# A recommendation model on one core: the last head in two halves, the last pairs in portions, spare matmuls behind the last products, and later waits for the gathers

## The chip, the core and the metric

The kernel runs on one core of one Trainium2 chip. A core has four engines that compute, each with its own stream of instructions: TensorE (PE), VectorE (DVE), ScalarE (ACT) and GpSimd (POOL). A fifth, SyncE (SP), only starts transfers here. They are kept in order by semaphores alone. The metric is the device time of one execution in microseconds (us). Before the change it is 152.27 us, the median of three runs (151.87 to 156.4).

## What is computed

512 samples each have 13 dense numbers and 26 table indices. Two dense layers make one vector of 128 from the dense numbers, a lookup in 26 tables makes 26 more. The dot products of all pairs of the 27 vectors, with the first vector itself, go through three layers to one probability. All is fp32.

```python
h = relu(dense_x @ bw1 + bb1)
x_bottom = relu(h @ bw2 + bb2)
sparse_embs = emb_tables[field_idx, sparse_x]
combined = concatenate([x_bottom[:, None, :], sparse_embs], axis=1)
interactions = einsum('bfd,bgd->bfg', combined, combined)
x_final = concatenate([x_bottom, interactions[:, rows, cols]], axis=-1)   # rows, cols: triu_indices(27, k=1)
t = relu(x_final @ tw1 + tb1)
t = relu(t @ tw2 + tb2)
return sigmoid(t @ tw3 + tb3)
```

## The kernel before

The 512 x 26 table rows are fetched in 104 chunks of 128 rows. Thirteen chunks make a group of 64 samples; there are 8 groups, 0 to 7, and `LAST` is 7. Two groups make a turn of 128 samples (`TURN`), and each turn ends in a head: layers 1 to 3.

**GpSimd** starts one indirect transfer per chunk, a gather, on line 189. Chunk c has its own place in `rows`, so no gather waits for a free buffer. Still, from chunk 4 on (`LEAD`) a gather waits until chunk c - 4 is transposed (line 188).

**PE** transposes each chunk through an identity (line 326) into one of two PSUM banks, `rows_T`; ahead of each transpose stands a matmul whose result is overwritten and never read (line 323). A group's 13 chunks are handled in units: 4, 3, 3, 3, and in the last group 4, 3, 3, 2, 1. Behind the transposes of a unit come the products of the unit before (`multiply`, line 342). One product takes a quad, 4 samples at once, 104 columns. A group has 16 quads in two batches of 8; batch h goes to `products[h]`, two PSUM banks of 4 quads each. An fp32 matmul shows as two passes in the trace, a transpose as one.

**DVE** copies the transposed chunks to `fields` (`fields_in`, line 224). The pairs, blocks of 32 partitions of the products, are brought to `pairs` by `take_pairs` (line 166) in 16 small copies per batch, 8 on DVE (quadrants 0 and 1) and 8 on ACT (quadrants 2 and 3). Three of four have 56 elements a partition, the fourth 40.

**The head** of a turn is layer 1 (line 351 for the dense vector, then 7 matmuls, line 357, with the pairs), `relu1` on ACT (271), layer 2 (366), `relu2` (277), layer 3 (372), `sigmoid` (283). The heads of turns 0 to 2 run inside the next turn's first group, layer 1 behind `multiply(group, 0)`. That of turn 3 stands behind all products. SP stores the 512 results when the last sigmoid is done.

Each engine runs its instructions strictly in the order in which its function below writes them. In the last group DVE takes the pairs of batch 0 between the fields of units 1 and 2 (lines 242 to 247).

Of the kernel before, what the change touches and what calls it, by code (L numbers as in the profile page):

```python
# [15 lines left out]
P = 128  # L16
BATCH = 512
# [40 lines left out]


TURN = 2 * GROUP  # L60


def evacuation_pieces(c0, c1):
# [29 lines left out]
def dlrm(nc, index_base, dense_bw1, weights, pair_weights, table, out):  # L93
# [7 lines left out]
    with ctx:  # L101
# [50 lines left out]

            return NU * group + u

        def take_pairs(copy, group, h, quadrants):

            src = products[h][:, :].rearrange("p (b c) -> p b c", c=BANK)[
                :, :, 0:BANK_QUADS * QUAD * SPARSE].rearrange(
                "p b (q s g) -> p s g b q", s=QUAD, g=SPARSE)
            a = group % 2  # L160
            dst = pairs[:, :, a * GROUP:(a + 1) * GROUP].rearrange(
                "p g (h b q s) -> p h s g b q", h=BATCHES, q=BANK_QUADS, s=QUAD)
            for s in quadrants:
                for j in range(SPLIT):
                    g0, g1 = j * PART, min((j + 1) * PART, SPARSE)
                    last = copy(dst[SLOT * j:SLOT * (j + 1), h, s, 0:g1 - g0],  # L166
                                src[SLOT * s:SLOT * (s + 1), s, g0:g1])
            return last

        block = ctx.enter_context(nc.Block())  # L170
# [1 line left out]
        @block.sync  # L172
        def _(sp):
            sp.dma_start(raw[:, :], index_base).then_inc(index_loaded, 16)
            sp.dma_start(w[:, :], weights).then_inc(weights_loaded, 16)
            sp.dma_start(wp[:, :, :], pair_weights).then_inc(pair_weights_loaded, 16)
            sp.wait_ge(probs_ready, ROUNDS)
# [15 lines left out]

        @block.vector
        def _(dve):
# [51 lines left out]
            pairs_in(LAST, 1)  # L247

        @block.scalar
        def _(act):  # L250
# [17 lines left out]
            def relu1(t):  # L268

                act.wait_ge(top1_made, t + 1)  # L270
                nc.scalar.activation(top1[:, :], top1_ps[:, 0:TURN], ACT.Relu,  # L271
                                     bias=w[:, TB1:TB1 + 1]).then_inc(top1_ready, 1)

            def relu2(t):

                act.wait_ge(top2_made, t + 1)
                nc.scalar.activation(top2[:, :], top2_ps[0:T2, 0:TURN], ACT.Relu,  # L277
                                     bias=w[0:T2, TB2:TB2 + 1]).then_inc(top2_ready, 1)

            def sigmoid(t):  # L280

                act.wait_ge(logits_made, t + 1)
                nc.scalar.activation(probs[:, t * TURN:(t + 1) * TURN], top2_ps[0:1, TURN:2 * TURN],  # L283
                                     ACT.Sigmoid, bias=w[0:1, TB3:TB3 + 1]).then_inc(probs_ready, 1)

            for t in range(ROUNDS):
# [4 lines left out]
                if t > 0:  # L291
                    sigmoid(t - 1)
                pairs_in(2 * t, 1)
                pairs_in(2 * t + 1, 0)
                pairs_in(2 * t + 1, 1)
            relu1(ROUNDS - 1)
            relu2(ROUNDS - 1)
            sigmoid(ROUNDS - 1)

        @block.tensor  # L300
        def _(pe):
# [9 lines left out]
                                       hidden[:, h, :], start=(h == 0), stop=(h == HH - 1))  # L311
            ins.then_inc(bottom_made, 1)

            def transposes(group, u):


# [3 lines left out]
                    pe.wait_ge(fields_ready, v - 1)  # L320
                for k in range(c0, c1):
                    c = group * GROUP_CHUNKS + k
                    nc.tensor.matmul(rows_T[v % 2][:, (k - c0) * P:(k - c0 + 1) * P], w[:, IDENT:IDENT + P],  # L323
                                     w[:, IDENT:IDENT + P], start=True, stop=True)
                    pe.wait_ge(gathered[c], 16)
                    nc.tensor.transpose(rows_T[v % 2][:, (k - c0) * P:(k - c0 + 1) * P],  # L326
                                              rows[:, c, :], w[:, IDENT:IDENT + P]).then_inc(transposed, 1)

            def multiply(group, u):

# [16 lines left out]
            def layer1(t):  # L347

                if t > 0:
                    pe.wait_ge(top1_ready, t)  # L350
                nc.tensor.matmul(top1_ps[:, 0:TURN], w[:, TW1X:TW1X + T1],  # L351
                                 fields[:, t * TURN:(t + 1) * TURN, 0], start=True, stop=False)
                for h in range(BATCHES):
                    pe.wait_ge(taken_dve[h], 2 * (t + 1))
                    pe.wait_ge(taken_act[h], 2 * (t + 1))
                for g in range(PART):
                    ins = nc.tensor.matmul(top1_ps[:, 0:TURN], wp[:, g, :], pairs[:, g, :],  # L357
                                           start=False, stop=(g == PART - 1))
                ins.then_inc(top1_made, 1)

            def layer2(t):

                pe.wait_ge(top1_ready, t + 1)
                if t > 0:
                    pe.wait_ge(probs_ready, t)
                nc.tensor.matmul(top2_ps[0:T2, 0:TURN], w[:, TW2:TW2 + T2], top1[:, :],  # L366
                                 start=True, stop=True).then_inc(top2_made, 1)

            def layer3(t):

                pe.wait_ge(top2_ready, t + 1)
                nc.tensor.matmul(top2_ps[0:1, TURN:2 * TURN], w[0:T2, TW3:TW3 + 1], top2[:, :],  # L372
                                 start=True, stop=True).then_inc(logits_made, 1)

            transposes(0, 0)
# [31 lines left out]
            layer3(ROUNDS - 1)  # L407


def pair_weight_order():  # L410
# [51 lines left out]
```

## Time and profile before

| | us |
|---|---|
| median of 3 runs | 152.27 |
| the profiled execution | 152.51 |
| its span, first to last instruction | 150.7 |
| PE busy / DVE / ACT / POOL | 106.8 / 56.8 / 39.5 / 98.7 |
| mean granted clock of PE | 0.909 of full |

Times in the trace count from the start of the span. Full speed of PE is 2.4 GHz, a granted clock of 0.50 is 1.2 GHz. PEld is the weight load of PE, which overlaps the matmuls. In a row of the timeline stand start, length, engine, line, operation, output and inputs with their shapes, how many instructions are merged, and in brackets how long the engine was idle before and who released it.

### The profile page before, as it was taken

How to read it: one execution, taken by the hardware profiler on the slowest of the kernel's cores; microseconds unless marked ns; L12 is line 12 of the kernel's file. 1: busy time of each engine (PE TensorE's matmuls, PEld its weight loads, DVE VectorE, ACT ScalarE, POOL GpSimd, SP SyncE). 2: the span in 40 equal slices, each digit the busy share in tenths (PEclk: the TensorE clock that was granted, in tenths of full speed). 3: DMA queues.
4: the chain of work that ended last, by engine and by line, in shares of the span. 5: the costliest groups of instructions: out<-in, count | busy, mean ns of one | idle time of the engine just before them, and what ended most of it. 6: DMA issues, size and time to landing. Idle time of an engine off the chain costs nothing.

```text
span 150.7 us, 1841 instructions
## 1 busy us (share of the span) xinstructions
PE 106.8 (71%) x656; PEld 87.6 (58%) x656; DVE 56.8 (38%) x219; ACT 39.5 (26%) x145; POOL 98.7 (65%) x108
## 2 busy tenths in 40 slices
PE   2993666656589978866666975566499969578682
PEld 1352555555459957755555954455498849468470
DVE  1702153262606261535326160716135442561600
ACT  3320031040404160313104160505013430450402
POOL 0727777777777777777777777777777777771000
PEclk9999999999955997799999999999959986975859
DMA  4311112221121222212121211221112122211000
GB/s 125 137 35 35 52 52 52 57 52 52 54 52 52 52 59 52 54 52 52 52 52 57 52 52 52 52 52 52 57 52 52 52 54 52 57 52 35 0 0 1
DMA packets 3797, 7.80 MB, mean 52 GB/s; under 512 B 1854, under 2 KB 1854, under 8 KB 3788
## 3 DMA queue, kind: packets, MB, share of 16 engines
q0 software_dynamic: 3328, 6.82, 17.2%
q1 hardware_dynamic: 434, 0.82, 1.8%
q8 instruction: 5, 0.08, 0.2%
q10 hardware_dynamic: 26, 0.04, 0.1%
q14 instruction: 4, 0.03, 0.1%
HBM read 7.67 MB, written 0.00 MB: 51 GB/s over the span
## 4 chain that ended last, share of the span: by engine, by line
POOL 41%; PE 23%; issue 15%; DMA 15%; DVE 3%; ACT 1%; DVEq 0%
POOL rows L189 41%; DMA rows<-table,row_index 14%; PE products L342 6%; PE top_ps L357 5%; PE rows_T L326 3%; PE rows_T L305 3%; PE rows_T L323 2%; PE products L310 2%; DVE pairs L166 2%; DMA db<-dense_bw 1%; DVE fields L224 1%; PE top_ps L351 1%; PE top_ps L372 0%; PE top_ps L366 0%; ACT top L271 0%
## 5 line engine op out<-in xcount | busy, mean ns | idle before, releaser
L189 POOL DMA_INDIRECT rows<-table,row_index x104 | 98.5, 947 | 37.4 <-issue 26.5
L326 PE MATMUL rows_T<-w,rows 128*128 128x128 f32 x104 | 34.5, 331 | 34.3 <-DMA rows<-table,row_index 33.9
L166 ACT COPY pairs<-products 32x56 f32<-32x56 f32 (+1 forms) x128 | 31.1, 243 | 82.1 <-PE products L342 80.8
L224 DVE COPY fields<-rows_T 128x494 f32<-128x494 f32 (+6 forms) x83 | 22.3, 319 | 73.9 <-PE rows_T L326 73.7
L323 PE MATMUL rows_T<-w 128*128 128x128 f32 x208 | 44.6, 308 | 0.0
L326 PEld LDWEIGHTS rows_T<-w,rows 128*128 128x128 f32 x104 | 16.3, 157 | 44.5 <-DMA rows<-table,row_index 44.3
L323 PEld LDWEIGHTS rows_T<-w 128*128 128x128 f32 x208 | 38.5, 228 | 1.0 <-issue 1.0
L342 PE MATMUL products<-fields 128*128 128x104 f32 x256 | 37.6, 294 | 2.0 <-DVE fields L224 2.0
L342 PEld LDWEIGHTS products<-fields 128*128 128x128 f32 x256 | 35.1, 211 | 4.3 <-DVE fields L224 3.0
L166 DVE COPY pairs<-products 32x56 f32<-32x56 f32 (+1 forms) x128 | 30.9, 241 | 9.1 <-PE products L342 7.2
L357 PE MATMUL top_ps<-pairs,wp 128*128 128x128 f32 x56 | 8.5, 313 | 1.9 <-DVE pairs L166 1.9
L357 PEld LDWEIGHTS top_ps<-pairs,wp 128*128 128x128 f32 x56 | 8.2, 226 | 2.3 <-issue 2.2
L305 PE MATMUL rows_T<-db 13*128 13x512 f32 x4 | 3.8, 1096 | 2.8 <-DMA db<-dense_bw 2.8
L271 ACT ACTIVATE top<-top_ps,w 128x128 f32<-128x128 f32 x4 | 1.5, 368 | 12.9 <-PE top_ps L357 12.9
L310 PE MATMUL products<-hidden,w 128*128 128x512 f32 x4 | 3.8, 1101 | 0.0
L305 PEld LDWEIGHTS rows_T<-db 13*128 13x128 f32 x4 | 1.2, 318 | 3.9 <-DMA db<-dense_bw 2.8
L310 PEld LDWEIGHTS products<-hidden,w 128*128 128x128 f32 x4 | 1.2, 324 | 2.5 <-issue 2.0
L351 PE MATMUL top_ps<-fields,w 128*128 128x128 f32 x8 | 2.4, 389 | 0.0
L283 ACT ACTIVATE probs<-top_ps,w 1x128 f32<-1x128 f32 x4 | 1.4, 358 | 3.6 <-PE top_ps L372 3.6
L213 DVE MEMSET fields<- 128x2560 f32 x1 | 2.2, 2192 | 0.5 <-issue 0.5
L277 ACT ACTIVATE top<-top_ps,w 64x128 f32<-64x128 f32 x4 | 1.4, 362 | 3.5 <-PE top_ps L366 3.5
L257 ACT ACTIVATE hidden<-rows_T,w 128x512 f32<-128x512 f32 x2 | 1.4, 688 | 3.1 <-PE rows_T L305 3.1
(16 smaller groups left out, 10.1 us busy)
## 6 DMA issues: line engine op xcount, KB each, us to landing
rows<-table,row_index POOLq DMA_INDIRECT x104, 2.5
wp<-pair_weights SPq DMA_DIRECT2D x1, 448.0 KB, 3.7
w<-weights SPq DMA_DIRECT2D x1, 291.5 KB, 3.0
raw<-index_base SPq DMA_DIRECT2D x1, 58.5 KB, 2.2
db<-dense_bw ACTq DMA_DIRECT2D x1, 39.0 KB
out<-probs SPq DMA_DIRECT2D x1, 2.0 KB
```

What stands on the lines that cost most here:

```text
L166: last = copy(dst[SLOT * j:SLOT * (j + 1), h, s, 0:g1 - g0], src[SLOT * s:SLOT * (s + 1), s, g0:g1])
L189: nc.gpsimd.indirect_dma_start(rows[:, c, :], None, table, bass.IndirectOffsetOnAxis(row_index[:, group, k:k + 1], 0)).then_inc(gathered[c ...
L213: nc.vector.memset(fields[:, :, SPARSE + 1:SLOT], 0.0)
L224: ins = nc.vector.tensor_copy(fields[:, b:b + n, 1 + f:1 + f + nf], rows_T[v % 2][:, col:col + n * nf].rearrange("p (n f) -> p n f", f=nf))
L271: nc.scalar.activation(top1[:, :], top1_ps[:, 0:TURN], ACT.Relu, bias=w[:, TB1:TB1 + 1]).then_inc(top1_ready, 1)
L305: nc.tensor.matmul(rows_T[h][:, 0:BATCH], db[:, BATCH + h * P:BATCH + (h + 1) * P], db[:, 0:BATCH], start=True, stop=True).then_inc(hidden ...
L310: ins = nc.tensor.matmul(products[0][:, 0:BATCH], w[:, BW2 + h * EMB:BW2 + (h + 1) * EMB], hidden[:, h, :], start=(h == 0), stop=(h == HH ...
L323: nc.tensor.matmul(rows_T[v % 2][:, (k - c0) * P:(k - c0 + 1) * P], w[:, IDENT:IDENT + P], w[:, IDENT:IDENT + P], start=True, stop=True)
L326: nc.tensor.transpose(rows_T[v % 2][:, (k - c0) * P:(k - c0 + 1) * P], rows[:, c, :], w[:, IDENT:IDENT + P]).then_inc(transposed, 1)
L342: ins = nc.tensor.matmul(products[h][:, col:col + n], four, four[:, :, 1:1 + SPARSE], start=True, stop=True)
L351: nc.tensor.matmul(top1_ps[:, 0:TURN], w[:, TW1X:TW1X + T1], fields[:, t * TURN:(t + 1) * TURN, 0], start=True, stop=False)
L357: ins = nc.tensor.matmul(top1_ps[:, 0:TURN], wp[:, g, :], pairs[:, g, :], start=False, stop=(g == PART - 1))
```

## The change

Four things. The wait of the gathers begins at chunk 8 instead of 4; it still asks for chunk c - 4. The heads are listed in `HEADS`: three of 128 samples, then one for group 6 and one for group 7, 64 samples each. Head 3 (group 6) now runs inside the last group: layer 1 behind the transposes of unit 1, layer 2 behind `multiply(LAST, 1)`, layer 3 behind `multiply(LAST, 2)`. In the last group, the pairs come in three steps: batch 0 whole, then the first bank of batch 1 (4 quads; one quadrant on DVE, three on ACT), then its second bank. And four matmuls that nobody reads stand behind the last products.

```diff
+HEADS = [(0, TURN), (TURN, 2 * TURN), (2 * TURN, 3 * TURN), (3 * TURN, 3 * TURN + GROUP),
+         (3 * TURN + GROUP, BATCH)]
...
-                if c >= LEAD:
+                if c >= 2 * LEAD:
                     pool.wait_ge(transposed, c - LEAD + 1)
...
+            def last_pairs_in(n, h, quadrants, b0, b1):
+
+                dve.wait_ge(multiplied, BATCHES * LAST + n)
+                take_pairs(nc.vector.tensor_copy, LAST, h, quadrants, b0, b1).then_inc(taken_dve[h], 1)
+
             fields_in(LAST, 1)
-            pairs_in(LAST, 0)
             fields_in(LAST, 2)
+            last_pairs_in(1, 0, (0, 1), 0, 2)
             fields_in(LAST, 3)
+            last_pairs_in(2, 1, (0,), 0, 1)
             fields_in(LAST, 4)
-            pairs_in(LAST, 1)
+            last_pairs_in(3, 1, (0, 1), 1, 2)
...
-            relu1(ROUNDS - 1)
-            relu2(ROUNDS - 1)
-            sigmoid(ROUNDS - 1)
...
+            relu1(3)
+            last_pairs_in(1, 0, (2, 3), 0, 2)
+            relu2(3)
+            sigmoid(3)
+            last_pairs_in(2, 1, (1, 2, 3), 0, 1)
+            last_pairs_in(3, 1, (2, 3), 1, 2)
+            relu1(4)
+            relu2(4)
+            sigmoid(4)
...
+            def keep_busy(spare, n):
+
+                for _ in range(n):
+                    nc.tensor.matmul(spare, w[:, IDENT:IDENT + P], w[:, IDENT:IDENT + P],
+                                     start=True, stop=True)
...
-                    if at == BATCH_QUADS - 1:
+                    if at == BATCH_QUADS - 1 or (group, h, at) == (LAST, 1, BANK_QUADS - 1):
                         ins.then_inc(multiplied, 1)
...
             multiply(LAST, 0)
             transposes(LAST, 1)
+            layer1(3)
             multiply(LAST, 1)
+            layer2(3)
             transposes(LAST, 2)
             multiply(LAST, 2)
+            layer3(3)
             transposes(LAST, 3)
             transposes(LAST, 4)
             multiply(LAST, 3)
             multiply(LAST, 4)
-            layer1(ROUNDS - 1)
-            layer2(ROUNDS - 1)
-            layer3(ROUNDS - 1)
+            keep_busy(rows_T[0][:, 0:P], 4)
+            layer1(4)
+            layer2(4)
+            layer3(4)
```

How this stands in the engines' streams. DVE, the end of the last group: `fields` copies come from `rows_T`, `pairs` copies from `products`. Before, from the fields of unit 1 on:

```order
L224 COPY fields<-rows_T 128x12
L166 COPY pairs<-products 32x7x8 x3
L166 COPY pairs<-products 32x5x8
L166 COPY pairs<-products 32x7x8 x3
L166 COPY pairs<-products 32x5x8
L224 COPY fields<-rows_T 128x14
L224 COPY fields<-rows_T 128x14x26
L224 COPY fields<-rows_T 128x6
L224 COPY fields<-rows_T 128x20
```

After, from the fields of unit 2 on:

```order
L227 COPY fields<-rows_T 128x6
L169 COPY pairs<-products 32x7x8 x3
L169 COPY pairs<-products 32x5x8
L169 COPY pairs<-products 32x7x8 x3
L169 COPY pairs<-products 32x5x8
L227 COPY fields<-rows_T 128x20
L227 COPY fields<-rows_T 128x9x26
L227 COPY fields<-rows_T 128x2
L169 COPY pairs<-products 32x7x4 x3
L169 COPY pairs<-products 32x5x4
L227 COPY fields<-rows_T 128x24
L227 COPY fields<-rows_T 128x4x26
```

The pairs of batch 0 moved from ahead of unit 2's fields to behind them, and four copies of half size stand between the fields of the last two units.

PE behind the last transpose of unit 1 in the last group (L342 of before and L372 of after are products, L323 and L342 of after the matmuls that nobody reads). Before:

```order
L326 MATMUL rows_T<-w,rows 128x128
L342 MATMUL products<-fields 128x104 x4
L323 MATMUL rows_T<-w 128x128
L326 MATMUL rows_T<-w,rows 128x128
L323 MATMUL rows_T<-w 128x128
```

After:

```order
L357 MATMUL rows_T<-w,rows 128x128
L383 MATMUL top_ps<-fields,w 128x64
L390 MATMUL top_ps<-pairs,wp 128x64 x7
L372 MATMUL products<-fields 128x104 x4
L400 MATMUL top_ps<-top,w 64x64
L342 MATMUL rows_T<-w 128x128
L357 MATMUL rows_T<-w,rows 128x128
```

Eight matmuls of layer 1 and one of layer 2 now stand ahead of the next transpose. The end of PE's stream, before:

```order
L326 MATMUL rows_T<-w,rows 128x128
L342 MATMUL products<-fields 128x104 x4
L351 MATMUL top_ps<-fields,w 128x128
L357 MATMUL top_ps<-pairs,wp 128x128 x7
L366 MATMUL top_ps<-top,w 64x128
L372 MATMUL top_ps<-top,w 1x128
```

And after:

```order
L357 MATMUL rows_T<-w,rows 128x128
L372 MATMUL products<-fields 128x104 x4
L342 MATMUL rows_T<-w 128x128 x4
L383 MATMUL top_ps<-fields,w 128x64
L390 MATMUL top_ps<-pairs,wp 128x64 x7
L400 MATMUL top_ps<-top,w 64x64
L407 MATMUL top_ps<-top,w 1x64
```

The head's matmuls are as many as before with half the columns, and four spare matmuls stand ahead of them.

## Rows read from the trace of the kernel before

**Rows 1.** The page, chain that ended last, share of the span by engine.

```profile
POOL 41%; PE 23%; issue 15%; DMA 15%; DVE 3%; ACT 1%; DVEq 0%
```

**Rows 2.** The list of waits, GpSimd: us in total, times, longest.

```profile
POOL rows L189 <- PE rows_T L326: 7.5, 16, 2.5
```

**Rows 3.** The timeline of the start: start, us, engine, line, operation, wait.

```profile
7.74 0.95 POOL L189 DMA_INDIRECT rows<-table,row_index  x1 [0.30 <-issue]
...
10.35 1.15 ACT L260 ACTIVATE fields<-products,w 128x512 f32<-128x512 f32 x1 [3.02 <-PE products L310]
...
11.18 0.95 POOL L189 DMA_INDIRECT rows<-table,row_index  x1 [2.50 <-PE rows_T L326]
...
13.74 0.33 PE L326 MATMUL rows_T<-w,rows 128*128 128x128 f32 x1 [1.61 <-DMA rows<-table,row_index]
```

**Rows 4.** The timeline in group 6, with the head of turn 2.

```profile
113.99 0.33 PE L326 MATMUL rows_T<-w,rows 128*128 128x128 f32 x1 [0.34 <-DMA rows<-table,row_index]
...
114.16 1.04 PE L342 MATMUL products<-fields 128*128 128x104 f32 x8
...
115.46 1.74 PE L357 MATMUL top_ps<-pairs,wp 128*128 128x128 f32 x14
...
117.26 0.27 PE L326 MATMUL rows_T<-w,rows 128*128 128x128 f32 x1
...
117.81 0.95 POOL L189 DMA_INDIRECT rows<-table,row_index  x1 [0.47 <-PE rows_T L326]
```

**Rows 5.** The timeline of the last group and the last head.

```profile
131.13 0.33 PE L326 MATMUL rows_T<-w,rows 128*128 128x128 f32 x1 [1.23 <-DMA rows<-table,row_index]
...
133.41 2.05 DVE L166 COPY pairs<-products 32x56 f32<-32x56 f32 x8 [1.23 <-PE products L342]
...
135.44 0.95 POOL L189 DMA_INDIRECT rows<-table,row_index  x1 [0.30 <-issue]
135.49 0.69 DVE L224 COPY fields<-rows_T 128x14 f32<-128x14 f32 x3
...
139.62 0.99 DVE L224 COPY fields<-rows_T 128x20 f32<-128x20 f32 x5 [3.44 <-PE rows_T L326]
...
140.23 1.22 PE L342 MATMUL products<-fields 128*128 128x104 f32 x8
...
141.49 2.01 DVE L166 COPY pairs<-products 32x56 f32<-32x56 f32 x8 [0.87 <-PE products L342]
...
143.76 3.25 PE L357 MATMUL top_ps<-pairs,wp 128*128 128x128 f32 x14 [1.87 <-DVE pairs L166]
147.05 0.37 ACT L271 ACTIVATE top<-top_ps,w 128x128 f32<-128x128 f32 x1 [3.55 <-PE top_ps L357]
...
147.47 0.43 PE L366 MATMUL top_ps<-top,w 128*64 128x128 f32 x2 [0.46 <-ACT top L271]
...
148.77 0.36 ACT L283 ACTIVATE probs<-top_ps,w 1x128 f32<-1x128 f32 x1 [0.47 <-PE top_ps L372]
```

**Rows 6.** Groups of instructions by shape: count, us busy, mean ns, idle before.

```profile
L166 DVE COPY pairs<-products 32x56 f32<-32x56 f32 x96 | 23.8, 248 | 8.7 <-PE products L342 7.2
...
L166 DVE COPY pairs<-products 32x40 f32<-32x40 f32 x32 | 7.1, 222 | 0.4
...
L257 ACT ACTIVATE hidden<-rows_T,w 128x512 f32<-128x512 f32 x2 | 1.4, 688 | 3.1 <-PE rows_T L305 3.1
...
L224 DVE COPY fields<-rows_T 128x24 f32<-128x24 f32 x1 | 0.2, 183 | 0.1
```

**Rows 7.** Stretches of the end: length, busy by engine, granted clock, DMA, GB/s.

```profile
133.70:140.40 6.70, 5.47 (x25) 4.67 (x24) 3.06 (x15) 1.69 (x7) 2.08 (x3) 0.50 0.12 29
130.20:133.60 3.40, 1.69 (x13) 1.50 (x14) 0.87 (x4) 0.19 (x1) 2.55 (x3) 1.00 0.21 57
140.50:143.80 3.30, 1.43 (x11) 1.07 (x11) 2.04 (x9) 1.93 (x8) 0.00 (x0) 1.00 0.00 0
143.90:147.00 3.10, 3.10 (x14) 2.82 (x14) 0.00 (x0) 0.00 (x0) 0.00 (x0) 0.50 0.00 0
```

More of the change, by code:

```diff
@@ L153, in unit_number, with take_pairs @@
             return NU * group + u
-        def take_pairs(copy, group, h, quadrants):
+        def take_pairs(copy, group, h, quadrants, b0=0, b1=BATCH_QUADS // BANK_QUADS):
             src = products[h][:, :].rearrange("p (b c) -> p b c", c=BANK)[
@@ L165, in take_pairs @@
                     g0, g1 = j * PART, min((j + 1) * PART, SPARSE)
-                    last = copy(dst[SLOT * j:SLOT * (j + 1), h, s, 0:g1 - g0],
-                                src[SLOT * s:SLOT * (s + 1), s, g0:g1])
+                    last = copy(dst[SLOT * j:SLOT * (j + 1), h, s, 0:g1 - g0, b0:b1],
+                                src[SLOT * s:SLOT * (s + 1), s, g0:g1, b0:b1])
             return last
@@ L176, in _ @@
             sp.dma_start(wp[:, :, :], pair_weights).then_inc(pair_weights_loaded, 16)
-            sp.wait_ge(probs_ready, ROUNDS)
+            sp.wait_ge(probs_ready, len(HEADS))
             sp.dma_start(out, probs[:, :]).then_inc(stored, 16)
@@ L266, in pairs_in, with relu1, relu2, sigmoid @@
                 take_pairs(nc.scalar.copy, group, h, (2, 3)).then_inc(taken_act[h], 1)
-            def relu1(t):
-                act.wait_ge(top1_made, t + 1)
-                nc.scalar.activation(top1[:, :], top1_ps[:, 0:TURN], ACT.Relu,
+            def relu1(i):
+                n = HEADS[i][1] - HEADS[i][0]
+                act.wait_ge(top1_made, i + 1)
+                nc.scalar.activation(top1[:, 0:n], top1_ps[:, 0:n], ACT.Relu,
                                      bias=w[:, TB1:TB1 + 1]).then_inc(top1_ready, 1)
-            def relu2(t):
-                act.wait_ge(top2_made, t + 1)
-                nc.scalar.activation(top2[:, :], top2_ps[0:T2, 0:TURN], ACT.Relu,
+            def relu2(i):
+                n = HEADS[i][1] - HEADS[i][0]
+                act.wait_ge(top2_made, i + 1)
+                nc.scalar.activation(top2[:, 0:n], top2_ps[0:T2, 0:n], ACT.Relu,
                                      bias=w[0:T2, TB2:TB2 + 1]).then_inc(top2_ready, 1)
-            def sigmoid(t):
-                act.wait_ge(logits_made, t + 1)
-                nc.scalar.activation(probs[:, t * TURN:(t + 1) * TURN], top2_ps[0:1, TURN:2 * TURN],
+            def sigmoid(i):
+                lo, hi = HEADS[i]
+                act.wait_ge(logits_made, i + 1)
+                nc.scalar.activation(probs[:, lo:hi], top2_ps[0:1, TURN:TURN + hi - lo],
                                      ACT.Sigmoid, bias=w[0:1, TB3:TB3 + 1]).then_inc(probs_ready, 1)
@@ L322, in transposes @@
                     c = group * GROUP_CHUNKS + k
-                    nc.tensor.matmul(rows_T[v % 2][:, (k - c0) * P:(k - c0 + 1) * P], w[:, IDENT:IDENT + P],
-                                     w[:, IDENT:IDENT + P], start=True, stop=True)
+                    block_T = rows_T[v % 2][:, (k - c0) * P:(k - c0 + 1) * P]
+                    keep_busy(block_T, 1)
                     pe.wait_ge(gathered[c], 16)
-                    nc.tensor.transpose(rows_T[v % 2][:, (k - c0) * P:(k - c0 + 1) * P],
-                                              rows[:, c, :], w[:, IDENT:IDENT + P]).then_inc(transposed, 1)
+                    nc.tensor.transpose(block_T, rows[:, c, :], w[:, IDENT:IDENT + P]).then_inc(transposed, 1)
             def multiply(group, u):
@@ L343, in multiply, with layer1 @@
                                            start=True, stop=True)
-                    if at == BATCH_QUADS - 1:
+                    if at == BATCH_QUADS - 1 or (group, h, at) == (LAST, 1, BANK_QUADS - 1):
                         ins.then_inc(multiplied, 1)
[L347 to L352, printed above, removed]
+            def layer1(i):
+                lo, hi = HEADS[i]
+                at = lo % TURN
+                if i > 0:
+                    pe.wait_ge(top1_ready, i)
+                nc.tensor.matmul(top1_ps[:, 0:hi - lo], w[:, TW1X:TW1X + T1],
+                                 fields[:, lo:hi, 0], start=True, stop=False)
@@ L353, in layer1 @@
                 for h in range(BATCHES):
-                    pe.wait_ge(taken_dve[h], 2 * (t + 1))
-                    pe.wait_ge(taken_act[h], 2 * (t + 1))
+                    takes = hi // GROUP + (hi == BATCH and h == 1)
+                    pe.wait_ge(taken_dve[h], takes)
+                    pe.wait_ge(taken_act[h], takes)
                 for g in range(PART):
-                    ins = nc.tensor.matmul(top1_ps[:, 0:TURN], wp[:, g, :], pairs[:, g, :],
+                    ins = nc.tensor.matmul(top1_ps[:, 0:hi - lo], wp[:, g, :], pairs[:, g, at:at + hi - lo],
```

26 lines of the change are left out of this document (16 added, 10 removed).

## The prediction

> **What bounds the kernel now.** I read the chain that ended last first, by engine: GpSimd (POOL) holds 41% of the span, its "issue" pauses and the transfers 15% each, PE 23% [rows 1]. So for most of the time the kernel runs at the pace at which GpSimd starts gathers. The list of waits has 7.5 us in which GpSimd waits for a transpose, in 16 waits, the longest 2.5 us [rows 2]. A pause of 0.30 stands between two gathers in any case (7.74 in [rows 3]), so those 16 cost 7.5 - 16 x 0.30 = 2.7 us, and 2.5 - 0.3 = 2.2 of it is one wait.
>
> The timeline of the start shows that wait: gather 3 starts at 7.74, gather 4 only at 11.18, released by the first transpose, which PE reaches after the bottom layers [rows 3]. All others together cost 0.5 us. The timeline of the end shows the other part that nothing hides: the last gather starts at 135.44, the last sigmoid ends at 149.13, 13.7 us later, though its rows are there some 2.5 us after its start [rows 5]. In that stretch I read who waits for whom: DVE takes out the pairs of batch 0 (133.41 to 135.46) before it takes the fields that PE needs (135.49), then come the last fields (139.62), products (140.23), 2.01 us of pairs on DVE and ACT, a layer 1 of 14 passes in 3.25 us at half the clock, and three short ACT steps.
>
> **The change part by part.** The sum is made against the profiled execution: 152.51 us, of which the span is 150.7 (0.24 above the median of the runs, 152.27).
>
> *GpSimd's waits.* Gathers 4 to 7 lose their wait. At the pace of 1.25 us (0.95 + 0.30) gather 4 starts at 7.74 + 1.25 = 8.99 instead of 11.18: 2.19 us earlier. Gather 8 then asks at 13.99 whether chunk 4 is transposed. Rows land about 2.55 us after the start (11.18 to 13.74 [rows 3]), so chunk 4 is there at 11.55; PE stood idle for 1.61 us ahead of 13.74, so it is free from 12.1 on at the latest, and ACT ends the bottom output at 11.50 [rows 3], so the transpose is done near 12.5, and gather 8 does not wait. The wait does not come back at once, and all later gathers keep their distances. **-2.19.** If it did come back, this part would be worth 0.
>
> *The head of group 6 inside the last group.* PE now runs layer 1 of 64 samples behind the transposes of chunks 95 to 97, ahead of the products, and layer 2 behind them. Its passes are no shorter: for 104 and 128 columns a pass takes about 0.11 us at full clock alike (8 in 1.04, 14 in 1.74 [rows 4]), where the columns alone would make a difference of a fifth. What they share is 128 columns of weights, and 64 samples don't change those, so I take 0.11 for 64 columns too. The same sequence stands in group 6: chunk 84 starts at 113.99, then products and layer 1, and chunk 85 starts at 117.26, 3.27 us later; gather 89 follows at 117.81, 0.55 behind [rows 4]. Here, moved up by 2.19: gather 97, six paces ahead of 135.44 - 2.19, starts at 125.75, its transpose at 128.30 (+2.55), chunk 98 at 128.30 + 3.27 + 0.22 (two short passes of layer 2, half of 0.43 [rows 5]) = 131.79, and gather 102, due at 132.00, can start at 131.79 + 0.55 = 132.34. So gathers 102 and 103 come 0.34 late: **+0.34**, and gather 103 starts at 133.59. In the other direction, were chunk 97 as late as in this profile (131.13 [rows 5] against gather 97 at 135.44 - 6 x 1.25 = 127.94, so 3.19), it would be +0.98; 0 if PE is a little quicker. Behind gather 102 only gather 103 is queued.
>
> *From the last gather to the last products.* Chunks 98 to 100 are transposed from 131.79 to 132.80, their fields (0.69) end at 133.53, and now the pairs of batch 0 follow them on DVE (2.05 [rows 5]) until 135.58. Then the next fields, 3 of the 5 copies that take 0.99 together, 0.6: 136.19. Then the new piece: 4 copies of 28 elements. The trace has none; the nearest are 0.222 us for 40 elements and 0.248 for 56 [rows 6]. A straight line through both gives 0.203 for 28. The lower bound is 0.183, a copy of 24 elements on 128 partitions; the upper is 0.248, no gain at all. I take the line with 0.01 between copies: 0.84, until 137.03. The last gather has landed at 136.14 and is transposed at 136.47, so its fields wait 0.56 for this piece; they take 0.38 and end at 137.42. Two quads of products are half of the 1.22 [rows 5] plus the drain, 0.70: 138.16. The last pairs start at 138.20, 4.61 behind gather 103, against 141.49 - 135.44 = 6.05: **-1.44**. It comes from the order of DVE and from PE at full clock. ACT has relu1 and the first pairs behind it by 133.6, relu2 by 134.0, sigmoid by 135.2, then 12 small copies (2.5) until 137.7: 0.5 us to spare. If layer 3 of group 6 slips by more than that, ACT is late next.
>
> *The last pairs.* 8 copies of 28 elements on each of DVE and ACT instead of 2.01: 8 x 0.21 = 1.68. **-0.33**, bounds -0.5 and 0.
>
> *The Trainium skill against this part.* The page "VectorE: DVE Perf Modes", section "The TRN2 errata", says that a small operation pays a fixed latency each time and that small tiles lose by it; its cycle table for PSUM to SBUF, used as an estimate, makes a copy of 28 elements 29 ns shorter than one of 56. By that the last pairs gain 0.23 instead of 0.33 and the piece ahead of the fields costs 0.9 instead of 0.84, so the sum would be 0.2 us higher. The two rows of the trace give the larger slope, and they decide.
>
> *The four unread matmuls.* 8 passes start behind the last products: 0.9 us at full clock, 1.7 at half (0.21 a pass, 14 passes in 3.25 less the drain [rows 5]). The pairs leave PE 1.68 + 0.26 us idle there (143.76 - 143.50 is the 0.26), so even the slow case is covered; without that cover it would cost 0.9. What they are worth is the clock of layer 1. It fell to its lower level, 1.2 GHz, at 143.8, after a stretch in which PE was busy 1.43 of 3.3 us; the fall before it, near 133.6, came after 1.69 of 3.4; and all 14 passes lie in the stretch of 0.50 behind it [rows 7]. In the changed kernel PE works from 136.1 to layer 1 at 140.14 for about 0.3 + 0.45 + 0.7 + 0.9 + 0.3 = 2.65 of 4.0 us, and nearly all the time before. I take it that the clock stays up: 14 passes in 1.74 instead of 3.25, **-1.51**.
>
> *The rest.* relu1, relu2 and sigmoid with 64 instead of 128 elements, layers 2 and 3 with 64 columns. From 147.05 to 149.13 it is 2.08 us; bounds are 2.08 and 1.5 (each of the five steps shortened by a third). ACT's 0.37 us for 128 elements [rows 5] against 0.688 for 512 [rows 6] is 0.83 ns an element, so 0.05 each; PE 0.07 each. **-0.30.**
>
> Sum: -2.19 + 0.34 - 1.44 - 0.33 - 1.51 - 0.30 = -5.43; 152.51 - 5.4 = 147.1, and against the median 0.2 less. I say **147.0 us**. The store behind the sigmoid stays.
>
> **The rivals.**
> - *The clock falls all the same before the last layer 1.* PE still has two gaps (0.5 before the last products, 1.1 before layer 1), and the fall at 143.8 came while it stood still for 1.87 [rows 5]. Then -1.51 is lost: 148.5.
> - *The early gathers give nothing.* GpSimd catches up until a later transpose holds it, or gather 8 waits as 4 did. Against it: at 13.99 chunk 4 has been transposed for 1.5 us, and PE has time ahead of it [rows 3]. Then 147.0 + 2.2 = 149.2.
> - *PE is somewhat late in the last group,* by late rows (3.19 instead of 2.55, twice) or a low clock in part of it: 148.5 to 151.
> - *Slower than before.* If the clock is low when layer 1 of group 6 begins, each pass is 0.21: 16 + 8 + 2 passes take 5.5 us instead of 3.2 ahead of chunk 98, gather 102 starts near 135.1 instead of 132.3, and the lag stays. With all passes of the end at 0.21 the last pairs start near 143.2 and end at 144.9, layer 1 at 148.4, the sigmoid at 150.3: 1.2 us behind the 149.13 of before, so 153.7. It passes the old time from a lag of about 5.4 us on, which only a low clock through nearly the whole last group gives. The profile has the lower clock from 133.7 to 140.4 [rows 7], but PE had half a stretch without work ahead of it, and now has more.
>
> **How the numbers follow.** The forecast 0.62 (its own range 146.1 to 148.0: copies and rest at their bounds, late rows once), clock falls 0.20, early gathers for nothing 0.07, PE late 0.08, slower 0.03. Two per cent, about what a measurement of this kernel can tell from no change, is a time below 149.2. Faster: 0.62 + 0.20 + half of the next, 0.85; same 0.12; slower 0.03. The range from 146.0 to 149.6 leaves out about 0.07 above (the slower case and half of PE late) and 0.08 below.
>
> **What the changed profile would show.** Gather 4 near 9.0 and gather 8 near 14.0 without a transpose as releaser; gather 103 near 133.6, with a wait of some 0.6 ahead of gather 102; small copies of 0.20; last pairs 4.6 us behind gather 103; 14 passes in 1.7 at a granted clock of 1.00. Wrong would be: a new wait at gathers 8 to 12, ACT ending the last pairs after DVE, or 0.50 in the last layer.

## The result

| | us, median (lowest to highest) | ratio to before, 95% interval |
|---|---|---|
| before, 4 runs | 152.19 (151.87 to 156.40) | |
| changed, 4 runs | 148.58 (147.40 to 150.55) | 0.974 (0.968 to 0.979) |
| its profiled execution | 148.02, span 146.2 | |

Ratios and their intervals take only the executions within 1.5% of the fastest of their kernel, medians and ranges take all. The change makes the kernel 2.6% faster. Forecast were 147.0 us, 146.0 to 149.6 and faster by over 2%. The profiled execution gained 4.5 us of the 5.4 in the sum.

The timeline of the changed kernel at the start, GpSimd's gathers 4 and 8 and the transpose of chunk 4:

```profile
8.90 0.94 POOL L192 DMA_INDIRECT rows<-table,row_index  x1 [0.30 <-issue]
...
12.78 0.27 PE L357 MATMUL rows_T<-w,rows 128*128 128x128 f32 x1
...
13.89 0.94 POOL L192 DMA_INDIRECT rows<-table,row_index  x1 [0.30 <-issue]
```

Gather 4 starts at 8.90 instead of 11.18 [rows 3], and gather 8 finds chunk 4 transposed 0.8 us earlier; neither waits. The list of waits, GpSimd's line (us in total, times, longest; before in [rows 2]):

```profile
POOL rows L192 <- PE rows_T L357: 6.4, 14, 1.4
```

Less 14 pauses of 0.30 that is 2.2 us, where the sum had 0.8 (0.5 left over from before and 0.34 new). The wait of 2.5 is gone, but others have grown. The end of the changed kernel, from the timeline:

```profile
129.29 0.33 PE L357 MATMUL rows_T<-w,rows 128*128 128x128 f32 x1 [1.20 <-DMA rows<-table,row_index]
...
129.66 1.69 PE L390 MATMUL top_ps<-pairs,wp 128*128 128x64 f32 x14
...
132.79 0.27 PE L357 MATMUL rows_T<-w,rows 128*128 128x128 f32 x1
...
133.34 0.94 POOL L192 DMA_INDIRECT rows<-table,row_index  x1 [1.35 <-PE rows_T L357]
...
134.59 0.94 POOL L192 DMA_INDIRECT rows<-table,row_index  x1 [0.31 <-issue]
...
137.21 0.80 DVE L169 COPY pairs<-products 32x28 f32<-32x28 f32 x4
...
138.05 0.35 DVE L227 COPY fields<-rows_T 128x24 f32<-128x24 f32 x2
...
139.19 1.67 DVE L169 COPY pairs<-products 32x28 f32<-32x28 f32 x8 [0.79 <-PE products L372]
...
141.12 1.75 PE L390 MATMUL top_ps<-pairs,wp 128*128 128x64 f32 x14 [0.83 <-DVE pairs L169]
142.90 0.31 ACT L281 ACTIVATE top<-top_ps,w 128x64 f32<-128x64 f32 x1 [2.05 <-PE top_ps L390]
...
144.30 0.30 ACT L295 ACTIVATE probs<-top_ps,w 1x64 f32<-1x64 f32 x1 [0.36 <-PE top_ps L407]
```

Against [rows 5]: the last gather starts at 134.59 (135.44 before), the last pairs 4.60 us behind it (6.05), they take 1.67 (2.01), layer 1 takes 1.75 (3.25), and from relu1 to the end of the last sigmoid it is 1.70 (2.08). Of the 2.2 us by which gather 4 starts earlier, 0.85 is left at the last gather. Two stretches of the end, columns as in [rows 7]:

```profile
137.10:141.10 4.00, 2.77 (x19) 2.31 (x20) 2.81 (x16) 3.08 (x16) 0.00 (x0) 1.00 0.00 0
```

```profile
139.90:142.90 3.00, 2.13 (x18) 1.83 (x16) 0.91 (x5) 0.90 (x5) 0.00 (x0) 1.00 0.00 0
```

PE is busy 2.77 of 4.0 us ahead of layer 1, and the granted clock stays at 1.00, 2.4 GHz.

### The profile page after: what moved, and what is told of

Its sections match the earlier page's. It is cut to its first block, busy times and chain, and to the rows that moved or that the text cites. A ratio compares the mean times of both kernels' runs of the same rounds, so it can differ in the third digit from the quotient of the medians.

```text
span 146.2 us, 1919 instructions
## 1 busy us (share of the span) xinstructions
PE 105.2 (72%) x684; PEld 87.3 (60%) x684; DVE 57.0 (39%) x223; ACT 42.1 (29%) x160; POOL 98.5 (67%) x108
## 4 chain that ended last, share of the span: by engine, by line
POOL 41%; PE 24%; DMA 15%; issue 15%; DVE 3%; ACT 1%; DVEq 0%
POOL rows L192 41%; DMA rows<-table,row_index 14%; PE products L372 8%; PE top_ps L390 5%; PE rows_T L342 4%; PE rows_T L357 4%; DMA raw<-index_base 1%; DVE pairs L169 1%; DVE fields L227 1%; PE top_ps L383 1%; PE top_ps L400 1%; PE top_ps L407 1%; ACT top L281 0%; ACT top L288 0%; ACT probs L295 0%
## 5 line engine op out<-in xcount | busy, mean ns | idle before, releaser
L357 PE MATMUL rows_T<-w,rows 128*128 128x128 f32 x104 | 33.6, 323 | 33.5 <-DMA rows<-table,row_index 33.4
L169 ACT COPY pairs<-products 32x56 f32<-32x56 f32 (+3 forms) x140 | 33.0, 236 | 71.3 <-PE products L372 69.9
L342 PE MATMUL rows_T<-w 128*128 128x128 f32 x216 | 44.1, 299 | 0.0
L342 PEld LDWEIGHTS rows_T<-w 128*128 128x128 f32 x216 | 38.1, 220 | 1.2 <-issue 1.0
L372 PE MATMUL products<-fields 128*128 128x104 f32 x256 | 37.0, 290 | 1.2 <-DVE fields L227 1.2
L372 PEld LDWEIGHTS products<-fields 128*128 128x128 f32 x256 | 34.4, 207 | 3.0 <-DVE fields L227 1.6
L169 DVE COPY pairs<-products 32x56 f32<-32x56 f32 (+3 forms) x132 | 31.3, 237 | 8.3 <-PE products L372 6.4
L390 PE MATMUL top_ps<-pairs,wp 128*128 128x128 f32 (+1 forms) x70 | 8.7, 275 | 0.8 <-DVE pairs L169 0.8
L281 ACT ACTIVATE top<-top_ps,w 128x128 f32<-128x128 f32 (+1 forms) x5 | 1.7, 346 | 15.0 <-PE top_ps L390 15.0
L295 ACT ACTIVATE probs<-top_ps,w 1x128 f32<-1x128 f32 (+1 forms) x5 | 1.7, 336 | 5.3 <-PE top_ps L407 5.3
L288 ACT ACTIVATE top<-top_ps,w 64x128 f32<-64x128 f32 (+1 forms) x5 | 1.7, 341 | 3.4 <-PE top_ps L400 3.4
L383 PE MATMUL top_ps<-fields,w 128*128 128x128 f32 (+1 forms) x10 | 2.6, 346 | 0.0
L400 PE MATMUL top_ps<-top,w 128*64 128x128 f32 (+1 forms) x10 | 2.0, 277 | 0.4 <-ACT top L281 0.4
```

The source lines that it names most:

```text
L169: last = copy(dst[SLOT * j:SLOT * (j + 1), h, s, 0:g1 - g0, b0:b1], src[SLOT * s:SLOT * (s + 1), s, g0:g1, b0:b1])
L342: nc.tensor.matmul(spare, w[:, IDENT:IDENT + P], w[:, IDENT:IDENT + P], start=True, stop=True)
L357: nc.tensor.transpose(block_T, rows[:, c, :], w[:, IDENT:IDENT + P]).then_inc(transposed, 1)
L383: nc.tensor.matmul(top1_ps[:, 0:hi - lo], w[:, TW1X:TW1X + T1], fields[:, lo:hi, 0], start=True, stop=False)
L390: ins = nc.tensor.matmul(top1_ps[:, 0:hi - lo], wp[:, g, :], pairs[:, g, at:at + hi - lo], start=False, stop=(g == PART - 1))
L400: nc.tensor.matmul(top2_ps[0:T2, 0:n], w[:, TW2:TW2 + T2], top1[:, 0:n], start=True, stop=True).then_inc(top2_made, 1)
```

## The experiments

The table has all runs. The kernel before was run beside each group; a ratio is to that. The three groups ran on three different chips, so ratios, and kernels of one group, are what to compare.

| kernel | group | us, median (range) | before in that group | ratio, 95% interval |
|---|---|---|---|---|
| before, later waits only | 1 | 151.17 (149.34 to 152.30) | 153.62 | 0.988 (0.979 to 0.998) |
| changed, no unread matmuls | 1 | 151.12 (147.48 to 155.12) | 153.62 | 0.974 (0.964 to 0.983) |
| changed, LEAD 8 | 1 | 146.53 (146.30 to 147.90) | 153.62 | 0.965 (0.958 to 0.971) |
| changed, samples shifted | 1 | 146.78 (one run) | 153.62 | |
| changed, LEAD 8, no unread matmuls | 2 | 148.48 (146.38 to 153.33) | 153.01 | 0.967 (0.957 to 0.978) |
| changed, LEAD 8, fields first | 2 | 146.32 (145.81 to 152.23) | 153.01 | 0.960 (0.957 to 0.964) |
| before, LEAD 8 | 2 | 148.66 (148.26 to 150.71) | 153.01 | 0.975 (0.971 to 0.979) |
| changed, again | 2 | 148.60 (147.05 to 152.25) | 153.01 | 0.974 (0.968 to 0.981) |
| changed, LEAD 8, whole last head | 3 | 169.06 (168.69 to 175.43) | 170.97 | 1.003 (0.998 to 1.008) |
| changed, LEAD 8, pairs as before | 3 | 173.21 (172.78 to 179.31) | 170.97 | 1.023 (1.016 to 1.030) |
| changed, LEAD 8, three more gathers | 3 | 182.71 (one run) | 170.97 | |
| before, LEAD 8, unread matmuls | 3 | 172.06 (170.56 to 173.63) | 170.97 | 1.013 (1.002 to 1.025) |

My theory was that of the prediction: the wait of gather 4, the order of DVE and the clock of the last layer 1 carry the gain. Two rivals had to be told from it: that the gathers' gain is given back at the heads, and that the unread matmuls do nothing for the clock.

**The later waits alone,** on the kernel before:

```diff
-                if c >= LEAD:
+                if c >= 2 * LEAD:
```

> The kernel before with one edit: the gathers wait from chunk 8 on instead of chunk 4. Theory: gather 4 starts near 8.9 instead of 11.18 and all later ones keep their distances, so the time falls by 2.2 us, to 150.0 (ratio 0.986). Rival 1: the gain is given back at the heads of turns 0 to 2, where PE then holds the gathers longer: gather 103 at 134.5 or later and a time of 151 to 152. Rival 2: the tail of the old order is not bound by the last gather (DVE takes the pairs of batch 0 first), so that part of the 2.2 us ends as a longer wait there: 151.

Measured 0.988, 1.8 us less with an interval from 0.4 to 3.2; the 2.2 us and both rivals lie in it. In its profile gather 4 starts at 8.96, but the last one at 135.46, as late as before. So in this execution the gain was given back, as rival 1 said, but not where it said: the holds at the heads are 0.11, 0.23 and 0.16 us (gathers 37, 63 and 89), those in the last group 1.14 and 1.33 (gathers 95 and 102). Its timeline:

```profile
131.22 2.04 PE L342 MATMUL products<-fields 128*128 128x104 f32 x8 [0.78 <-DVE fields L224]
...
134.21 0.94 POOL L189 DMA_INDIRECT rows<-table,row_index  x1 [1.63 <-PE rows_T L326]
```

The products of the last group run at half the clock here (2.04 us for 8 passes, 1.14 at full clock), the transpose behind them is late, and gather 102 waits 1.63. No layer 1 stands there in this kernel. The wait for chunk c - 4 turns a slow stretch of PE into a late gather, whatever makes PE slow.

**LEAD 8 in the changed kernel:**

```diff
-LEAD = 4
+LEAD = 8
...
-                if c >= 2 * LEAD:
+                if c >= LEAD:
                     pool.wait_ge(transposed, c - LEAD + 1)
```

> The changed kernel with LEAD 8: a gather waits for chunk c - 8 instead of c - 4. Theory: the holds of the gathers (0.26, 0.19, 0.15, 0.49 and 1.05 us beyond the pause of 0.30, 2.1 in all) are gone, gather 103 starts near 132.5 instead of 134.59; PE then has a backlog in the last group, so only about half of it, 1.0 us, reaches the end: 147.6. Rival 1: all 2.1 us reach the end, 146.5. Rival 2: PE is what bounds the last group, the last gather has nothing to do with it, and the time stays at 148.6 within 0.3.

146.53 us and a ratio of 0.965, against 148.6 and 0.974 for the change itself: by the medians rival 1, and not my half; by the ratios it is 1.4 us, between the two. Each chunk has its own place in `rows`, so nothing but the order of waits is lost. GpSimd's waits, and the end of the timeline:

```profile
POOL rows L192 <- PE rows_T L357: 4.0, 13, 0.3
```

```profile
132.52 0.94 POOL L192 DMA_INDIRECT rows<-table,row_index  x1 [0.30 <-PE rows_T L357]
...
137.65 1.66 DVE L169 COPY pairs<-products 32x28 f32<-32x28 f32 x8 [0.78 <-PE products L372]
...
139.56 1.75 PE L390 MATMUL top_ps<-pairs,wp 128*128 128x64 f32 x14 [0.82 <-DVE pairs L169]
...
142.75 0.30 ACT L295 ACTIVATE probs<-top_ps,w 1x64 f32<-1x64 f32 x1 [0.36 <-PE top_ps L407]
```

No wait is longer than the pause. The last gather starts 2.07 us earlier than in the changed kernel, and the last sigmoid ends 1.55 earlier: in this pair of profiles 0.5 goes into PE's backlog, a quarter, where I had expected half. The median gains 2.1, and five of six executions lie between 146.30 and 146.74. That the executions with longer holds are gone fits this, but only one execution has a profile.

**The changed kernel without its unread matmuls:**

```diff
-            keep_busy(rows_T[0][:, 0:P], 4)
             layer1(4)
```

> The changed kernel without the four unread matmuls behind the last products. Theory: PE works less ahead of the last layer 1, the granted clock falls to 0.50 before it, its 14 passes take 3.2 us instead of 1.75, and the time is 1.5 us longer (150.1 against 148.6). Rival: the earlier work of the last group (head 3, products without a gap) already holds the clock, the passes take 1.75 us and the time is the same within 0.3 us. Between: the clock falls in a part of the executions only, and the mean is 0.5 to 1 us longer.

The times scatter from 147.5 to 155.1, and the ratio of 0.974 is that of the changed kernel: the times do not show the 1.5 us. Its profile is of a long execution (span 151.4) and shows two things. The last layer 1 takes 3.22 us, and one of the holds is seen at its full size. The timeline at the head of turn 1, and the stretch around it:

```profile
81.65 2.46 PE L390 MATMUL top_ps<-pairs,wp 128*128 128x128 f32 x14
...
84.72 0.94 POOL L192 DMA_INDIRECT rows<-table,row_index  x1 [2.15 <-PE rows_T L357]
```

```profile
79.00:86.00 7.00, 6.76 (x41) 6.43 (x42) 1.37 (x6) 0.73 (x2) 3.81 (x5) 0.70 0.15 40
```

At 1.2 GHz through the products and part of layer 1, PE is busy for 6.76 of 7.0 us and still reaches chunk 59 so late that gather 63 is held 1.85 us. At the next head it is 1.78. These two holds, 3.6 us, are most of the 5.7 us that this execution (153.2) has over the shortest (147.5).

**The same with LEAD 8:**

> The changed kernel with LEAD 8 and without the four unread matmuls, beside the one with LEAD 8 alone (146.5 us, 146.3 to 147.9). With LEAD 8 the times scatter little, so this tells what the unread matmuls are worth. Theory: the clock falls ahead of the last layer 1, its 14 passes take 3.22 instead of 1.75 us and the small matmuls of layers 2 and 3 0.2 more, so 148.1 in most executions. Rival: the profile without them and with LEAD 4 had its low clock from an earlier delay; here the clock stays up, 14 passes take 1.75 and the time is 146.5 within 0.3.

148.48 us, beside 146.32 of the kernel with them in the same group (which also has the fields first, worth at most 0.7 of it, below). The intervals of the two ratios overlap (0.957 to 0.978, 0.957 to 0.964), and against LEAD 8 with them in the other group (0.965) it is 0.4 us, so the totals don't settle it. The profile does for one execution:

```profile
139.62 2.62 PE L390 MATMUL top_ps<-pairs,wp 128*128 128x64 f32 x14 [1.72 <-ACT pairs L169]
```

```profile
136.00:139.60 3.60, 1.49 (x10) 1.15 (x11) 2.43 (x13) 2.73 (x14) 0.00 (x0) 1.00 0.00 0
139.60:142.20 2.60, 2.58 (x14) 2.46 (x14) 0.00 (x0) 0.00 (x0) 0.00 (x0) 0.63 0.00 0
```

The first stretch again, in the profile with LEAD 8 and the unread matmuls:

```profile
136.00:139.60 3.60, 2.37 (x19) 2.04 (x18) 2.37 (x13) 2.66 (x14) 0.00 (x0) 1.00 0.00 0
```

Up to layer 1 the two profiles agree within 0.07 us. Then PE, busy 1.49 of 3.6 us here and 2.37 there, has its clock lowered in layer 1, and the 14 passes take 2.62 instead of 1.75. So the work of head 3 alone does not hold the clock; how much of the 1.5 us is lost depends on when it falls.

**The kernel before with LEAD 8:**

> The kernel before with one edit, LEAD 8 (a gather waits for chunk c - 8). Theory: the kernel before loses more to holds of its gathers than the 2.2 us at gather 4, and most of what differs between its executions (151.3 to 155.4) comes from them: a low clock at a head makes PE late and PE holds the gathers. So gather 103 starts at 132.5 in every execution, the scatter shrinks below 1.5 us, and the time is 149.5 to 150. Rival: the scatter comes from the last group, behind the last gather; then it stays at 3 us or more and the median gains 2.2 only.

148.66 us, less than I expected: 3.9 us under before by the ratio, 4.4 by the medians. Five of six executions lie between 148.26 and 149.60. One number in one line gives as much as the whole change (0.975 and 0.974 in the same group), so the holds behind gather 4 cost the old kernel nearly as much as the 2.2 us of the one at gather 4. The profile read for the prediction [rows 2] had only 0.5 us of them. The end of its timeline:

```profile
132.54 0.94 POOL L189 DMA_INDIRECT rows<-table,row_index  x1 [0.30 <-PE rows_T L326]
...
138.52 2.00 DVE L166 COPY pairs<-products 32x56 f32<-32x56 f32 x8 [0.79 <-PE products L342]
140.78 3.33 PE L357 MATMUL top_ps<-pairs,wp 128*128 128x128 f32 x14 [1.85 <-ACT pairs L166]
...
145.86 0.36 ACT L283 ACTIVATE probs<-top_ps,w 1x128 f32<-1x128 f32 x1 [0.47 <-PE top_ps L372]
```

The last layer 1 has the low clock, as in [rows 5]. By the ratios of two groups, the three other edits are worth 1.0% on top of LEAD 8 (0.965 against 0.975), 1.5 us, with intervals that just touch. In these two profiles the part from the last gather to the last sigmoid is 13.68 and 10.53 us, 3.15 less: twice as much. The profile here is of the second longest of six executions (149.60), and no trace shows whether the shorter ones had the low clock in their last layer 1 too. So the 3.15 us are shown for the profiled executions alone, and by the ratios the gain at the end is smaller.

**The changed kernel again:**

> The changed kernel once more, on the same chip as the others. Theory: 148.6 within 1 us, with executions from 147 to 151, and holds of the gathers in the profile that add up to 1 to 4 us, the longer ones at chunks 63 and 89 where a low clock meets a head. Against the kernel with LEAD 8 (146.5) it shows what the wait for chunk c - 4 still costs: 2 us at the median.

148.60 us. Its profile is of its shortest execution (147.05). The holds add up to 1.0, the lower bound of what I expected, with 0.2 and 0.1 at chunks 63 and 89, since no low clock met a head there:

```profile
132.14 0.94 POOL L192 DMA_INDIRECT rows<-table,row_index  x1 [0.73 <-PE rows_T L357]
...
133.38 0.94 POOL L192 DMA_INDIRECT rows<-table,row_index  x1 [0.30 <-issue]
...
137.99 1.65 DVE L169 COPY pairs<-products 32x28 f32<-32x28 f32 x8 [0.78 <-PE products L372]
```

Here gather 102 is held 0.43 us and the last gather starts at 133.38. That is the execution the prediction described (0.34 and 133.59, and a time of 147.0).

**The fields ahead of the small copies, with LEAD 8:**

```diff
-            last_pairs_in(2, 1, (0,), 0, 1)
             fields_in(LAST, 4)
+            last_pairs_in(2, 1, (0,), 0, 1)
```

> The changed kernel with LEAD 8, and on DVE the fields of the last unit ahead of the four small pair copies. Theory: the last fields wait 0.8 us behind those copies (136.51 instead of 135.75 in the profile with LEAD 8), PE waits 0.41 for them; now the last products end 0.7 earlier, ACT with its 12 copies becomes late by 0.15, and the last pairs start 0.5 earlier: 146.0. Rival: ACT, not DVE, decides when the last pairs start, and the time stays at 146.5 within 0.2.

```profile
135.16 0.81 DVE L227 COPY fields<-rows_T 128x20 f32<-128x20 f32 x5 [0.36 <-PE rows_T L357]
135.77 1.14 PE L372 MATMUL products<-fields 128*128 128x104 f32 x8 [0.31 <-DVE fields L227]
...
136.95 1.65 DVE L169 COPY pairs<-products 32x28 f32<-32x28 f32 x8 [0.25 <-PE products L372]
138.91 1.75 PE L390 MATMUL top_ps<-pairs,wp 128*128 128x64 f32 x14 [0.87 <-ACT pairs L169]
```

The last products run in one piece, DVE starts the last pairs 0.70 earlier than with LEAD 8 alone, and layer 1 starts 0.65 earlier, with ACT as the last to finish. The median is 146.32 against 146.53 in the other group, the ratio 0.960 against 0.965; the intervals overlap, so the gain is shown in the profile and not in the time. It is the fastest kernel of the study: 4% under the kernel before, 1.4% under the changed one by the ratios (0.960 and 0.974, same group). It is also 1.4% under the old kernel with LEAD 8 of that group (0.975), and here the intervals are apart (0.957 to 0.964, 0.971 to 0.979): the edits at the end, with the fields first, gain time beyond the wait.

**The shifted samples:**

```diff
-    index = np.asarray(r_sparse_x).reshape(chunks, P).T
+    index = np.roll(np.asarray(r_sparse_x), -GROUP, axis=0).reshape(chunks, P).T
```

(the dense inputs and the output are shifted alike)

> The changed kernel with the samples in another order: shifted by one group of 64, so chunk c fetches the table rows that chunk c + 13 fetched. Both traces have late landings at the same chunks (37, 38, 79, 90 and 97: 3.2 to 3.9 us after the start of the gather instead of 2.5). If the lateness belongs to the rows that are fetched, it moves to chunks 24, 25, 66, 77 and 84, and chunk 97 lands 2.5 us after its start, with gather 102 held 0.4 instead of 1.05 us. If it belongs to the place in the program, it stays at 37, 38, 79, 90 and 97. If it is chance, there is no pattern.

The late chunks stayed: 37 at 3.07, 38 at 3.38, 79 at 3.86 and 90 at 3.55 us; 24, 25, 66, 77 and 84 did not take their place, save 25, which had been 2.8 to 2.9 before. Chunk 97 was not late this time; it was in four of the ten profiles of before, the changed kernel and the first two groups. Chunk 79 in this kernel, its gather and its transpose:

```profile
102.88 0.94 POOL L192 DMA_INDIRECT rows<-table,row_index  x1 [0.30 <-issue]
...
106.74 0.33 PE L357 MATMUL rows_T<-w,rows 128*128 128x128 f32 x1 [1.90 <-DMA rows<-table,row_index]
```

In the kernel before it is 105.14 and 109.06. So in this kernel the lateness of 37 and 79 belongs to a place in the program, not to the rows that are fetched and not to a time.

**The third group** stands apart: the kernel before itself took 170.97 us there.

> The changed kernel with LEAD 8 and three more gathers ahead of chunk 0, one at a time, into a tile that nobody reads (they cost about 8 us at the start). With LEAD 8 the late landings stood at chunks 21, 37 and 79 in every profile, also with other rows. If they belong to the place in GpSimd's queue, they move to chunks 18, 34 and 76. If they belong to the place in PE's stream, they stay at 21, 37 and 79.

> The changed kernel with LEAD 8 and the last head whole again (128 samples behind all products), pairs in portions and the unread matmuls kept. Theory: splitting the head saves only 0.3 us behind the last layer 1, whose passes are as long with 64 columns as with 128, and it costs PE 1.9 us of work ahead of the last group's products, of which 0.6 reaches the last pairs. Whole, the last pairs start near 137.0 instead of 137.65, 14 passes take 1.75, and the time is 146.2 against 146.5. Rival: the work of head 3 is what keeps the clock up in the last group; without it the last layer 1 or the products ahead of it run at half the clock: 147.7 or more.

> The changed kernel with LEAD 8 and the pairs of the last group as before the change (batch 0 ahead of the fields of unit 2, batch 1 whole at the end). Theory from the profiles: the last pairs take 2.0 instead of 1.66 us, but nothing stands between the fields of the last two units, so they start 0.8 earlier: the time falls by 0.4, to 146.1. Rival, from the prediction: DVE holds the fields of unit 2 behind the pairs of batch 0 and everything behind comes later, so the time rises by 0.5 to 1.5, to 147 to 148.

> The kernel before with LEAD 8 and the four unread matmuls behind its last products, beside the kernel before with LEAD 8 alone (148.5, where the last layer 1 took 3.33 us at half the clock). Theory: they hold the clock through the wait for the pairs, 14 passes take 1.75 us, and the time is 147.0. Rival: PE's gap in that order (2.3 us of pairs, less 0.9 to 1.7) is still too long, the passes take 3.3 and the time is 148.5.

Every one of these profiles has 9 to 13 gaps of 1.6 to 5.3 us in PE's stream, where the changed kernel's has 3. The last gather starts at 152.6 or later though GpSimd had LEAD 8, and beyond its pauses GpSimd is held about 20 us in all (2.7 in [rows 2]). The first large gap, in the old kernel with LEAD 8 and unread matmuls (`remote` stands where the profile found no instruction that released the engine):

```profile
17.78 0.33 PE L326 MATMUL rows_T<-w,rows 128*128 128x128 f32 x1 [0.79 <-DMA rows<-table,row_index]
...
25.00 0.69 DVE L224 COPY fields<-rows_T 128x14 f32<-128x14 f32 x3 [7.13 <-remote]
25.09 2.01 ACT L166 COPY pairs<-products 32x56 f32<-32x56 f32 x8 [13.61 <-remote]
25.13 0.94 POOL L189 DMA_INDIRECT rows<-table,row_index  x1 [2.72 <-remote]
...
25.74 1.61 PE L342 MATMUL products<-fields 128*128 128x104 f32 x6 [3.73 <-DVE fields L224]
```

The same transpose, of chunk 9, and the same copy in the old kernel with LEAD 8 of the second group:

```profile
17.77 0.33 PE L326 MATMUL rows_T<-w,rows 128*128 128x128 f32 x1 [0.65 <-DMA rows<-table,row_index]
...
18.14 0.69 DVE L224 COPY fields<-rows_T 128x14 f32<-128x14 f32 x3 [3.09 <-PE rows_T L326]
```

DVE's copy of chunks 7 to 9 starts 7.2 us behind the start of their last transpose, not 0.37, and DVE has stood idle for 7.13. ACT and GpSimd, which wait for PE too, go on within 0.13 us of it, and PE, which needs that copy, at 25.74. As the rows stand, the others learn late that PE is done, and PE then has to wait for them. Why, no run tells. So the totals can't answer what was asked: whether the split of the head and the portions gain anything at the usual pace stays open. The places of the late landings were not settled by the kernel with three more gathers either. Two things can still be read. With LEAD 8, the split head and the unread matmuls, the kernel with pairs as before took 173.2, and the one with a whole last head and the new pairs 169.1; the two edits differ by 4 us there and aren't told apart. And the last layer 1 of the old order with the four unread matmuls behind its products, timeline and stretch:

```profile
164.75 1.80 PE L357 MATMUL top_ps<-pairs,wp 128*128 128x128 f32 x14 [0.99 <-DVE pairs L166]
```

```profile
164.70:166.50 1.80, 1.75 (x14) 1.64 (x14) 0.00 (x0) 0.00 (x0) 0.00 (x0) 1.00 0.00 0
```

1.80 us at full clock, behind 2.04 us of pairs, where it took 3.33 behind 2.00 without them. That agrees with the theory and does not show it: these are profiles of two groups, one execution each, and the clock had risen 2.7 us ahead of layer 1 here and 3.6 us ahead there, so it may have stayed up without them.

## Why the prediction was right, point by point

- **GpSimd's waits, -2.19.** Right: gather 4 at 8.90 (8.99 expected), gather 8 at 13.89 without a wait (13.99), and alone it measured 1.8 us (0.4 to 3.2). But at the last gather 0.85 us of it is left in the profile of the change, and nothing in that of the waits alone: the holds of the next point take it back.
- **"All later gathers keep their distances", and +0.34 for head 3.** This is the step that was mis-sized. In the profiled execution gather 102 was held 1.05 us, gather 95 0.49 and gather 37 0.26; all holds are 2.1 us where the sum had 0.8 (0.34, and 0.46 carried over from before), and the last gather started at 134.59 instead of 133.59. Chunk 97 came late again (3.24 us), which was named as the bound of +0.98. The second profile has 0.43 and 133.38. The sum was made against a quiet execution of before and took its holds for the usual ones; LEAD 8 shows what they are worth: 1.4 us by the ratios and 2.1 by the medians in the changed kernel, and in the old one 1.7 and 2.2 beyond the 2.2 of gather 4.
- **From the last gather to the last pairs, -1.44.** Right in size: 4.60 in the first profile, 4.61 in the second, 4.61 expected. The small copies took 0.80 (0.84), and the fields of the last unit waited for them, as expected; the experiment with the fields first takes that wait away. How much is the order of DVE and how much PE's clock is not shown. With LEAD 8 this part is 5.98 us in the old kernel, with a granted clock of 0.52 from 133.0 to 137.4, and 5.13 in the changed one at full clock; the run with the pairs as before, which should have told, fell into the third group.
- **The last pairs, -0.33.** Right: 1.67 (1.68). The straight line through two rows was nearer than the cycle table of the Trainium skill ("VectorE: DVE Perf Modes", "The TRN2 errata"), by which it would have been 1.78; the trace has more cost per element than that table. The fixed cost of each copy, which the table has too, shows: half the elements, four fifths of the time (0.20 and 0.248 us).
- **The clock, -1.51.** Right: 1.75 at 1.00. That the unread matmuls do it is shown, in one execution each, by the two profiles with LEAD 8 that differ in them alone up to there (1.75 and 2.62). What they are worth in the time is not shown: nothing with LEAD 4 and 0.4 us with LEAD 8 by the ratios, 2.0 to 2.5 us by medians that scatter, all across groups, and at most 2.2 in one group.
- **The passes with 64 columns.** Right: 14 in 1.69, against 1.74 with 128 [rows 4]. Half the columns save 0.05 us in all.
- **The rest, -0.30.** 1.70 instead of 1.78: -0.38.

The time of 148.6 lies 1.6 above the forecast and outside the forecast's own range (146.1 to 148.0). It is the time of the third rival, PE late in the last group (148.5 to 151), which got 0.08: all five profiles in which the gathers wait for chunk c - 4 from chunk 8 on have holds, 0.9 to 4.8 us in all. The forecast of 147.0 was that of an execution with little of it, and that the range held is owed to the room it left for such rivals.

## What to carry to other kernels

A wait that protects nothing (each chunk has its own buffer here) should be as loose as it can be; set tight to the steady state, it hands slow moments of the consumer to the producer that bounds the kernel. One line, LEAD 8, gave as much as the whole change. No run left the wait out altogether. A profile is one execution: where slack is a few tenths of a microsecond, ask what the waits would be with the consumer at half its clock, and add that to the sum. Where TensorE idles ahead of the last short chain, a few unread matmuls can hold its clock, if another wait hides them; look for the gain in the time too, for here it shows in the profile alone.

## What the runs showed of the hardware

Rows land late at the same few chunks: chunk 37 is transposed 3.1 to 3.6 us after the start of its gather and chunk 79 after 3.3 to 3.9, instead of 2.5, in all ten profiles of the kernel before, the changed kernel and the first two groups, with other rows fetched and with the start of the gather moved by more than 2 us. It is the transfer that lands late and not PE that starts late, since the trace has the landing by itself. Gather 79 of the changed kernel:

```profile
DMA to landing us min/median/max: 3.5/3.5/3.5
```

In the ten profiles the landing of chunk 37 stands 3.0 to 3.6 us behind the start of its gather and that of chunk 79 3.2 to 3.9, where the median of all gathers is 2.5, and both transposes start 0.04 us behind it. Chunks 21 and 60 land late in nine of the ten (3.4 to 4.3). Why these chunks stays open.

In the third group, on another chip, the same kernel ran 12% slower (171 against 152 to 154 us), with GpSimd at the same pace (1.25 us a gather) when it was not held, and with PE gaps of 2 to 5 us about ten times per execution. In the rows above the other engines go on up to 7 us after the work of PE that they wait for. No run tells why.
